# Cross-attention with a mixture of experts: where the products of probabilities and values stand in TensorE's order

## What is computed

```
q, k, v  = LN(x) Wq' + bq,  ctx Wk' + bk,  ctx Wv' + bv        # 16 heads of 16
probs    = softmax(clip(q k' / 4, -50, 50), masked)            # 56 x 1500 for each head
probs   /= probs.sum() + 1e-8
delta    = LN(clip(residual_scale) * ((probs v) Wo' + bo)) * gamma + beta
x1       = x + tanh(g_xattn) * delta
logits   = LN(x1) w_router ; the two largest, softmax of them
out      = x1 + tanh(g_ffn) * sum_e w_e * (relu(LN(x1) w_fc[e])^2 w_proj[e])
```

## Time and profile before

| | before |
|---|---|
| median of 3 runs | 1228.75 us (1228.09 to 1229.5) |
| the profiled execution: its own time, its span | 1228.58 us, 1226.4 us |
| TensorE busy, weight loads busy | 1192.0 us (97%), 1149.7 us (94%) |
| VectorE busy | 855.7 us (70%) |
| ScalarE busy | 684.9 us (56%) |
| GpSimd busy | 144.1 us (12%) |
| `pv`, L497: matmul records, mean | 12288, 214 ns |
| scores, L482, each of three forms | 1536 records, 267 to 270 ns |
| v, L456, each of three forms | 1520 records, 278 to 285 ns |
| k, L459, each of three forms | 760 records, 385 to 403 ns |
| mean granted clock of TensorE | 0.996 of full |

### The profile page before, as it was taken

How to read it: one execution, slowest core, us unless ns; L and a number is a source line. 1 busy time by engine, 2 the same in 40 slices (tenths; PEclk the granted TensorE clock), 3 DMA queues, 4 the chain that set the end, 5 groups by cost and what they waited for, 6 DMA issues and landing times. The chain is left out here.

```text
span 1226.4 us, 56179 instructions
## 1 busy us (share of the span) xinstructions
PE 1192.0 (97%) x25428; PEld 1149.7 (94%) x25428; DVE 855.7 (70%) x1715; ACT 684.9 (56%) x838; POOL 144.1 (12%) x142
## 2 busy tenths in 40 slices
PE   6899999999999999999999999999999999999998
PEld 6899999999999999999999999999999999899998
DVE  5567777767777777676767777677767676788555
ACT  3466565656565656565655665565656555534443
POOL 0000000000000000000000000000000010244443
PEclk9899999999999999999999999999999999999999
DMA  4122121222221212121222211222212120210000
GB/s 144 57 65 68 53 71 65 67 69 67 68 67 40 91 44 81 55 74 46 69 67 70 67 61 60 67 67 69 65 39 78 55 71 29 66 28 10 18 10 18
DMA packets 36858, 72.87 MB, mean 59 GB/s; under 512 B 11221, under 2 KB 20754, under 8 KB 36626
## 3 DMA queue, kind: packets, MB, share of 16 engines
q1 hardware_dynamic: 27746, 58.57, 15.8%
q10 hardware_dynamic: 8880, 10.75, 2.6%
HBM read 64.48 MB, written 3.90 MB: 56 GB/s over the span
## 5 line engine op out<-in xcount | busy, mean ns | idle before, releaser
L687 ACT ACTIVATE prob<-sc_ps,m_bias 125x896 f32<-125x896 f32 x384 | 377.3, 1009 | 336.8 <-PE sc_ps L482 336.4
L456 PE MATMUL v_ps<-wv_hi,c_hi 64*125 64x256 f32 x1520 | 312.2, 285 | 2.7 <-DVE c_lo L846 2.6
L459 PE MATMUL k_ps<-c_hi,wk_hi 64*128 64x500 f32 x760 | 306.2, 403 | 0.0
L456 PE MATMUL v_ps<-wv_lo,c_hi 64*125 64x256 f32 x1520 | 302.3, 278 | 0.9 <-issue 0.9
L456 PE MATMUL v_ps<-wv_hi,c_lo 64*125 64x256 f32 x1520 | 301.6, 278 | 0.0
L459 PE MATMUL k_ps<-c_lo,wk_hi 64*128 64x500 f32 x760 | 293.5, 386 | 0.5 <-issue 0.5
L459 PE MATMUL k_ps<-c_hi,wk_lo 64*128 64x500 f32 x760 | 293.0, 385 | 0.0
L855 DVE TENSOR_TENSOR vst<-v_ps,rowv 125x512 f32<-125x512 f32 x191 | 131.4, 688 | 212.8 <-PE v_ps L456 212.8
L992 DVE TENSOR_SCALAR prob<-prob 125x896 f32<-125x896 f32 x384 | 235.6, 620 | 36.1 <-ACT prob L687 36.0
L456 PEld LDWEIGHTS v_ps<-wv_hi,c_hi 64*125 64x125 f32 x1520 | 226.7, 184 | 16.3 <-issue 5.8
L482 PE MATMUL sc_ps<-q_lo,kh 64*125 64x224 f32 x1536 | 233.2, 270 | 0.6 <-issue 0.5
(11 more groups left out here) (133 smaller groups left out, 1956.3 us busy)
## 6 DMA issues: line engine op xcount, KB each, us to landing
raw<-in_ctxT SPq DMA_DIRECT2D x96, 500.0 KB, 3.6
w_raw<-in_we ACTq DMA_DIRECT2D x16, 256.0 KB, 3.9
rec<-inv_scratch SPq DMA_DIRECT2D x64, 56.0 KB, 2.0
xq<-in_x ACTq DMA_DIRECT2D x16, 112.0 KB, 2.9
xr<-in_x ACTq DMA_DIRECT2D x16, 112.0 KB, 3.7
x_scratch<-x ACTq DMA_DIRECT2D x16, 112.0 KB, 3.7
out_y<-acc SPq DMA_DIRECT2D x7, 256.0 KB, 2.0
acc<-x_scratch SPq DMA_DIRECT2D x1, 1280.0 KB, 6.1
```

What stands on the lines that cost most here:

```text
L456: v_last = pe.matmul(v_ps[0:TC, j * D:(j + 1) * D], c_s[v_rows, cs], w_m[v_rows, k, :], start=begin and j == 0, stop=end, skip_group_check ...
L459: k_last = pe.matmul(k_ps[:, half, 0:TG], w[k_rows, k, ws], c_m[k_rows, :], start=begin, stop=end)
L687: act.activation(prob[0:TC, c % PB, :].rearrange("p (c n) -> p c n", c=2), sc_ps[0:TC, 2 * (c % 2):2 * (c % 2) + 2, 0:NH * S // 2], ACT.Ex ...
```

## The change

Of the four `pv` at the head of a group the first two stay there. The other two, for chunks c-2 and c-1, go behind the scores of chunk c+1. Nothing else is edited.

```
@@ -554,9 +554,12 @@
                     more = not (final and q == PG - 1)
                     if first and q == 1:
                         pe.wait_ge(o_clear, 1)
-                    if not (first and q == 0):
-                        for d in range(GC, 0, -1):
-                            pv(*((i, c - d) if q > 0 else (i - 1, PC - d)))
+                    def pv_two(d):
+                        if not (first and q == 0):
+                            for d in (d, d - 1):
+                                pv(*((i, c - d) if q > 0 else (i - 1, PC - d)))
+
+                    pv_two(GC)
                     beside_pv(i, q, first, late, final)
                     if more:
                         kv_part(n, 0, slot, 0)
@@ -566,6 +569,7 @@
                     if first and q == 0:
                         pe.wait_ge(v_evac, 2)
                     scores(i, c + 1)
+                    pv_two(2)
                     scores(i, c + 2)
                     if more:
                         kv_part(n, 1, slot, 0, freed.get(q, ()))
```

## The result

The changed kernel takes 1337.51 us (median of 4 runs, 1337.28 to 1338.04), against 1228.42 us for the kernel before (1227.92 to 1229.5). The ratio is 1.0882, 95% interval 1.0869 to 1.0896. The forecast was 1338, in a range of 1302 to 1366.

What follows compares the result with a forecast made beforehand. TensorE's own instruction list was taken as the bound. 7.50 us per pair over fifteen pairs, corrected to 110.6, plus 5 for the first pair, less 6 of holes, gave 109.6 on 1228.58: 1338 us, own range 1312 to 1361, overall 1302 to 1366.

Steps and rivals of the forecast that it cites:

- the holes won back: TensorE waits ahead of pv without a releaser, 14.5 us in the kernel before: 6 us of them taken off.
- Step 1: One more pv entry and exit in each of 95 groups: 0.28 us each, 26.6 us alone; second block 1.08 us.
- Step 2: Group head, q=0, 1, 2: the shorter block no longer covers vst, part A waits 0.17 us; +0.45 us each.
- Step 4: VectorE's o_ps copy waits for the later pv, vst queued behind: part C waits 2.20 us (q=3), 1.11 (q=0).
- (3): Heads of q=3 and q=5: the small work waits for kl, +1.10 us and +0.72 us.
- Step 5: Head of q=4: VectorE is still behind, so the head lasts 1.63 us instead of 1.69; +1.02 us in all.
- Rival C: Blocks of 32 matmuls free of 14.5 us of holes, if entry and exit cost under 0.15: 1214 us; chance 0.03.
- Rival A: Only the added pv entries and exits count, other waits hidden, most holes won back: 1244 us; chance 0.07.
- Rival B: Clock falls to 1.2 GHz in the holds, 1.75 us each: 1364 us, 1390 with short ones; chance 0.13.

Runs made afterwards that it cites:

- E6: E1 with its later two pv split, one behind the scores of c+1 and one behind those of c+2: 1307.05 us, ratio 1.0618.
- E1: The changed kernel with VectorE's copy of o_ps moved behind the clip of chunk c+1, at q = 0 and q = 3: 1278.35 us, ratio 1.0404.
- E7: The kernel before, all four pv at the head, with VectorE's copy of o_ps moved behind the clip of c+1: 1230.13 us, ratio 0.9998.
- E10: The changed kernel with the later o_ps copy at q = 3 alone: 1296.24 us, ratio 1.0523.
- E2: The kernel before with pv split two and two at q = 0 and q = 3 only: 1320.55 us, ratio 1.074.
- E4: The kernel before with three pv left at the head and one behind the scores of c+1: 1322.52 us, ratio 1.0764.
- E9: The changed kernel with the later o_ps copy at q = 0 alone: 1330.77 us, ratio 1.0806.
- E5: The kernel before with three pv at the head, one behind the scores of c+1, and the later o_ps copy: 1252.66 us, ratio 1.0178.
- E3: The kernel before with pv split two and two at q = 1, 2, 4, 5 only: 1276.83 us, ratio 1.0385.

## Why the prediction was right, step by step

The time was met to 0.5 us, and part of that is luck: the sizes of the steps were some 7 us too small, the holes won back 8 too few, and one fall of the clock, 1 us, stood in no term. Per pair, by the undisturbed pair of 71.86 against 63.88:

| step | forecast | measured |
|---|---|---|
| second block between the scores (1) | 1.08 | 1.12: 0.77 + 0.91 + 0.75 for scores, block, scores, less 1.31 |
| q = 1, q = 2 (2) | +0.45 each | +0.54, +0.57 |
| q = 0 with its hold (2, 4) | +1.56 | +1.77; the hold itself 1.11 |
| q = 3 with its hold (3, 4) | +3.30 | +3.38; the hold itself 2.20 |
| q = 4 (5) | +1.02 | +0.97 |
| q = 5 (3) | +0.72 | +0.76 |
| sum | 7.50 | 7.99 |

Step 1 was read off a neighbour of another kind and held: 0.31 instead of 0.28, near the 0.30 of E6. Step 2 was 0.1 short, since part A starts 0.14 behind the end of `vst` instead of 0.05, and behind each hold part C runs 0.09 slower. Step 4, the largest, came out exact by two errors of 0.10 that cancel: from the end of `vst` to part C pass 0.15 and not 0.05 (283.32 to 283.47), and from the end of the block to part C TensorE has 0.75 of its own and not 0.65, since the exit counted in step 1 was left out here. E1, E7 and E10 show its mechanism and not only its size: the wait goes when the copy leaves its place ahead of `vst`, and nothing happens when the same move is made where no `pv` was moved. Step 5 follows from it; E10 takes both away together. Together the sizes cost 15 x 0.49 = 7 us more than forecast. The ends of the range 1312 to 1361 are not the sums of the terms given for them, which would be 1303 and 1365; the measured time lies well inside both.

The holes were mis-sized the other way: I gave back 6 us and all 13 to 14 were won. Rival C had blocks of 32 free of holes, and was right in it; it fell by its own condition, an entry and exit under 0.15, where the entries and exits alone cost 95 x 0.31 = 29 us, twice the holes. Rival A fell with the two holds. Rival B was right in kind for one pair of the changed kernel; I had argued that 2.2 us is too short a wait for the clock to fall, and E2, E4 and E9 show that it is long enough in some places and not in others. That the changed kernel met only one fall is luck. Its fall made q = 3 longer by 1.56 and q = 4 shorter by 0.57, about 1 us, as in E9, so 14 more would be an estimated 14 us; the range would have held that too.

## What to carry to other kernels

Before moving an instruction that another engine waits for, read that engine's queue behind the waiting instruction: here the price was not the wait of the copy, which nobody needed soon, but `vst` queued behind it, and moving the copy behind `vst`, `kl` and two clips took 59 of the 109 us away. A block that looks like mere work may be the cover of a chain on other engines: measure the chain from the block's start, and a block can be shortened down to that length (three `pv`, 1.29 against 1.15) and no further. And count switches: with TensorE at 97%, each added change between kinds of matmul was paid in full.

## What the runs showed of the hardware

- An added run of column-strip `pv` between row-halved scores costs 0.28 to 0.33 us (E6 against E1, 95 times; E5's group against the one before), besides its matmuls.
- TensorE's holes without a releaser end 1.2 to 1.6 us after a packet of the queue q8 "instruction" and lie multiples of 252 matmul records, two packets' worth, apart (kernel before, E2, E3). They were seen in kernels with runs of 64 short matmuls, in the kernel before from about 440 us on: after 105 to 124 of 128 records, later also behind the run; in E2 after 84 to 124. Kernels whose runs are of 16 and 32 matmuls had none, those of 48 hardly any (about 1 us in all in E5), and leaving only some long runs made the holes larger, up to 2.0 us a block (E3).
- The granted clock fell to 1.2 GHz for some microseconds behind waits of TensorE of 2.20 us in none of 11 cases (changed kernel), in 8 of 11 (E2), 10 of 11 (E4) and 10 of 11 (E9); once behind one of 1.80 and once behind one of 1.90, and in E3 behind two holes of 1.5 and 2.0. Behind waits of 1.1 us it never fell (E10, 15 times). A fall makes the group 1.4 to 1.6 us longer. What decides between them is open.
